# Expert weights split during the feed-forward groups and kept in DRAM, and routing in three batches with row transfers from inside the block

## What is computed

```python
x = x + ffn0(attn0(x))           # L0: 16-head cosine attention; relu^2 feed-forward, 5 spiking steps
X = attn1(x)                     # L1: 16-head attention with a bias, layernorm behind it
X = X + attn_block(rmsnorm(X, g1)) # 4 heads, one shared key and value head
nx = rmsnorm(X, g2);  xf = nx.reshape(-1, d)
rw = softmax(xf @ Wr.T + expert_bias)
topw, topi = top_k(rw, 2);  topw = softmax(topw)
shared = swiglu(xf, sW1, sW2, sW3)
h  = silu(einsum('td,efd->etf', xf, eW1)) * einsum('td,efd->etf', xf, eW3)
eo = einsum('etf,edf->etd', h, eW2)
out = x + X + shared + combine(topw, topi, eo)
```

## Time and profile before

| | us |
|---|---|
| median of three runs | 1443.55 (1443.48 to 1451.34) |
| the profiled execution, as timed | 1444.31 |
| its span, first to last instruction | 1442.6 |
| TensorE busy in the span | 1299.9 (90%) |
| VectorE, ScalarE, GpSimd busy | 1035.3, 896.2, 710.8 |
| DRAM read and written in the span | 39.47 MB, 24.02 MB |

### The profile page before, as it was taken

The page is one execution under the profiler, slowest core; times in us unless marked ns, Lnnn a source line. Parts: engine busy times, 40 slices in busy tenths (PEclk is TensorE's granted clock), DMA queues, the critical chain, the costliest instruction groups (busy, mean ns, idle before and its releaser), DMA issues.

```text
span 1442.6 us, 43140 instructions
## 1 busy us (share of the span) xinstructions
PE 1299.9 (90%) x15310; PEld 1147.9 (80%) x15311; DVE 1035.3 (72%) x2129; ACT 896.2 (62%) x2309; POOL 710.8 (49%) x797
## 2 busy tenths in 40 slices
PE   4899999999689999889999999689998689999990
PEld 4799999998579999778888888568877578888870
DVE  4798988888736555787887787778887576555546
ACT  3676777767356666656666676477776254555545
POOL 2556565564435454445445444367766662333330
PEclk9899999999799999999999999899999899999995
DMA  8200000001030000000000000020001623333319
GB/s 230 54 9 10 8 11 8 8 10 38 2 87 1 1 0 1 3 10 10 9 8 10 9 8 13 21 58 15 16 15 63 221 87 116 104 104 101 103 42 349
DMA packets 87021, 71.15 MB, mean 49 GB/s; under 512 B 49981, under 2 KB 80831, under 8 KB 85824
## 3 DMA queue, kind: packets, MB, share of 16 engines
q1 hardware_dynamic: 80320, 51.73, 12.6%
q0 software_dynamic: 6528, 17.05, 3.3%
HBM read 39.47 MB, written 24.02 MB: 44 GB/s over the span
## 4 chain that ended last, share of the span: by engine, by line
PE 53%; issue 21%; POOL 10%; DVE 9%; ACT 4%; another core or an unknown queue 1%; DMA 1%; DVEq 0%; ACTq 0%; POOLq 0%; SPq 0%
PE psQ L2332 8%; PE psQ L1946 7%; PE psW L2024 7%; PE psW L2311 5%; POOL pn L758 5%; PE psQ L2137 3%; POOL rq L784 3%; PE psS L2137 3%; PE psW L2125 3%; PE psM L2125 3%; PE psS L2048 2%; PE psT L1975 2%; PE psT L2059 2%; PE psM L1998 2%; PE psT L2319 2%
## 5 line engine op out<-in xcount | busy, mean ns | idle before, releaser
L1946 PE MATMUL psQ<-xT,wq 128*128 128x256 f32 x1536 | 225.2, 298 | 3.5 <-ACT cur L1114 1.8
L1946 PEld LDWEIGHTS psQ<-xT,wq 128*128 128x128 f32 x1536 | 205.3, 201 | 4.5 <-issue 2.5
L2024 PE MATMUL psW<-wout,oT 128*128 128x256 f32 x1536 | 205.5, 292 | 1.1 <-ACT oT L977 1.1
L2024 PEld LDWEIGHTS psW<-wout,oT 128*128 128x128 f32 x1536 | 194.3, 197 | 1.3 <-ACT oT L977 1.3
L2332 PE MATMUL psQ<-W,exT 128*128 (+1 forms) x624 | 171.2, 410 | 0.0
L758 POOL TENSOR_TENSOR pn<-ex,rden 128x1024 f32<-128x1024 f32 x64 | 124.5, 1945 | 43.5 <-DVE rden L1437 43.5
L977 ACT ACTIVATE oT<-psT,small 128x512 fp32r<-128x512 f32 x128 | 81.1, 685 | 91.3 <-PE psT L2059 91.2
L802 POOL TENSOR_TENSOR hT<-hf,hT 128x512 fp32r<-128x512 f32 x64 | 85.9, 1341 | 102.1 <-ACT hT L1110 101.9
L912 POOL DMA_INDIRECT results<-result,idx x72 | 70.1, 974 | 133.7 <-ACT result L1241 128.7
L770 POOL TENSOR_TENSOR masked_bias<-bias_t,negmask 128x1024 f32<-128x1024 f32 x32 | 68.9, 2152 | 132.5 <-DVE ex L1405 132.5
L1364 DVE SCALAR_TENSOR_TENSOR oT<-psT,small,oT 128x512 fp32r<-128x512 f32 x128 | 90.2, 746 | 55.9 <-ACT oT L977 55.9
(11 more groups left out here) (302 smaller groups left out, 3374.6 us busy)
## 6 DMA issues: line engine op xcount, KB each, us to landing
rows<-sorted SPq DMA_DIRECT2D x72, 132.0 KB, 2.1
both<-results SPq DMA_DIRECT2D x8, 1024.0 KB, 11.8
raw_w<-W SPq DMA_DIRECT2D x27, 256.0 KB, 3.8
vv<-vp SPq DMA_DIRECT2D x256, 16.0 KB, 1.8
out<-X SPq DMA_DIRECT2D x8, 512.0 KB, 8.8
X<-x SPq DMA_DIRECT2D x1, 3584.0 KB, 18.4
bvv<-v_all SPq DMA_DIRECT2D x128, 16.0 KB, 1.8
sorted<-rows SPq DMA_DIRECT2D x9, 132.0 KB
```

The costliest lines, as they stand in the source:

```text
L1946: mm = nc.tensor.matmul(psQ[:, cc, h * QT:h * QT + QT], wq[w][:, k, c * P:c * P + P], xT[g % 2][u][:, k, :], start=(k == 0 and j == 0), st ...
L2024: mm = nc.tensor.matmul(psW[:, 0:D], oT[u][:, c, :], wout[w][:, c, :], start=(u == 0 and c == 0 and w == 0), stop=(u == 1 and c == CH - 1))
```

## The change

Four things are changed.

**The weights are split early.** The 27 thirds ("pieces") of the nine experts are split on VectorE, both halves, at the end of each of the first six feed-forward groups, 4, 5, 5, 5, 4 and 4 pieces (PARKED). SyncE loads a raw piece (256 KB) into one of four buffers and, once VectorE has split it, writes both halves (512 KB) to the DRAM tensor `parked`; it waits until that write has landed before it loads the next piece into the same buffer. VectorE waits once for all pieces, at the start of the last group. VectorE's loop over the groups is written out. The raw buffers lie in places that the feed-forward doesn't use.

**The experts are loaded split.** `load_expert` is one transfer of 1.5 MB in place of three of 256 KB. Experts 0 and 1 are loaded one after the other, SyncE waiting for the first to land before it goes on to the block's value rows. The 54 split instructions are gone from the block and the shared expert, on ScalarE and VectorE.

**Three batches.** Tiles 0 to 11 are chosen at steps 22 and 23, ranked on TensorE within step 25, ahead of the output product of tile 19 in the same PSUM bank psW, and placed at 25; tiles 12 to 23 at 34, 35, 37 and 37; tiles 24 to 31 at 41, 42, 43 and 44. TensorE's next output product waits until VectorE has read the ranks (`r_read`).

**Row transfers from step 26 on.** One send a step for 14 steps, then the other 50 one after another, held to the shared expert's transposes by `(t - 7) * 8 // 7 + 1`. GpSimd's and VectorE's block loops are written out for it.

```diff
-BATCHES = ((0, 20), (20, TILES))
-FIRST_CHOICE, SECOND_CHOICE, RANK, PLACES = (-6, 5), (-5, 6), (-2, 7), (-1, 8)
-SENT_AHEAD = 3
+BATCHES = ((0, 12), (12, 24), (24, TILES))
+FIRST_CHOICE, SECOND_CHOICE, PLACES = (-14, -2, 5), (-13, -1, 6), (-11, 1, 8)
+RANKED_BEFORE, RANK = (19, 31), 7
+SEND_STEP, SENT_IN_BLOCK = 26, 14
...
-SPLIT_STEP = [-4, -3, -2, 0, 1, 2, 3, 4, 5] + list(range(10, 28))
+PARKED = [4, 5, 5, 5, 4, 4, 0]
+PIECES = KD + 1
...
+            def load_piece(n):
+                p, part = divmod(n, PIECES)
+                raw = raw_piece[n % 4][:, 1, :]
+                got = sem(f"p_raw{n % 4}")
+                if part < KD:
+                    for j, w in enumerate(("W1", "W3")):
+                        sp.dma_start(raw[:, j * D:j * D + D], a[w][p, part * P:part * P + P, :]).then_inc(got, 16)
+                else:
+                    sp.dma_start(raw.rearrange("p (k n) -> p k n", k=KD), a["W2"][p].rearrange("(k p) n -> p k n", p=P)).then_inc(got, 16)
+            def park(n):
+                p, part = divmod(n, PIECES)
+                sp.wait_ge(sem("p_lo"), n + 1)
+                sp.dma_start(parked[p, :, :, part * 2 * D:part * 2 * D + 2 * D], piece[n % 4][:].bitcast(F32)).then_inc(sem("p_kept"), 16)
+                sp.wait_ge(sem("p_kept"), 16 * (n + 1))
+            for n in range(4):
+                load_piece(n)
+            for n in range(PIECES * EP):
+                park(n)
+                if n + 4 < PIECES * EP:
+                    load_piece(n + 4)
             spread_v(LAYERS[1], load_block)
...
+                sp.dma_start(W[:, slot, :, :].bitcast(F32), parked[p]).then_inc(done, 16)
             sp.wait_ge(sem("t_oev"), 2 * TILES)
-            for p in range(2):
-                load_expert(p, SHARED_SLOT + p, sem("e_first"))
+            load_expert(0, SHARED_SLOT, sem("e_weights"))
+            sp.wait_ge(sem("e_weights"), 16)
+            load_expert(1, SHARED_SLOT + 1, sem("e_weights"))
...
-            for p in (3, EP - 1, EP - 2):
-                load_expert(p, (p + 1) % EP, sem("e_rest"))
-            for p in range(4, EP - 2):
-                load_expert(p, p + 1, sem("e_last"))
+            for p in range(3, EP):
+                load_expert(p, (p + 1) % EP, sem("e_weights"))
...
-                if t >= SENT_AHEAD:
-                    pool.wait_ge(sem("e_xTp"), t - SENT_AHEAD + 1)
-                for k in range(TOP_K):
-                    send(t, k)
-            pipeline(pool, block_step, 1, 4, 10, numbers)
+                if n >= SENT_IN_BLOCK and k == 0:
+                    pool.wait_ge(sem("e_xTp"), (t - SENT_IN_BLOCK // TOP_K) * 8 // 7 + 1)
+                send(t, k)
+            for i in range(1, TILES + 10):
+                block_step(i, i % 2)
+                numbers(i)
...
+            def split_piece(n):
+                part = n % PIECES
+                hi, lo = piece[n % 4][:, 0, :], piece[n % 4][:, 1, :]
+                raw = raw_piece[n % 4][:, 1, :]
+                dve.wait_ge(sem(f"p_raw{n % 4}"), (0 if n % 4 else 16) + sum(16 if m % PIECES == KD else 32 for m in range(n % 4, n + 1, 4)))
+                if part < KD:
+                    then(nc.vector.tensor_scalar(hi, raw, g2col[:, part:part + 1], None, ALU.mult))
+                    ins = nc.vector.scalar_tensor_tensor(lo, raw, g2col[:, part:part + 1], hi.bitcast(F32), ALU.mult, ALU.subtract)
...
             ffn_in_lo(0, 0)
+            for g in range(GROUPS):
+                ffn(g, g % 2, first=g == 0, last=g == GROUPS - 1)
+                if g < GROUPS - 1:
+                    for n in range(sum(PARKED[:g]), sum(PARKED[:g + 1])):
+                        split_piece(n)
```

More of the change, by code:

```diff
@@ L335, in build @@
         count = sb("ffn_work", "count", [P, G4 * D], BF16)
+        pieces_at = (place["xT"][0] - 8 * K, place["ffn_work"][0])
+        piece = [nc.alloc_sbuf_tensor_at(f"piece{i}", [P, 2, 2 * D], F32R, offset=pieces_at[i // 2] + 4 * K * (i % 2)) for i in range(4)]
+        raw_piece = [nc.alloc_sbuf_tensor_at(f"raw_piece{i}", [P, 2, 2 * D], F32, offset=pieces_at[i // 2] + 4 * K * (i % 2)) for i in range(4)]
         place["ffn_work"][0] += 8 * K
@@ L407, in build @@
         row_place = sb("route", "row_place", [P, TOP_K, TILES], I32)
-        next_row = [sb("route", f"next_row{i}", [P, E], F32) for i in range(3)]
+        next_row = [sb("route", f"next_row{i}", [P, E], F32) for i in range(4)]
         blank_at = sb("route", "blank_at", [P, E], I32)
@@ L1246, in expert_step @@
                     nc.scalar.activation(ehT[0][:], psT[:, 0, 0:D].rearrange("p (k q) -> p k q", q=P), ACT.Copy).then_inc(sem("e_hhi"), 1)
-            def first_half(i):
-                for piece in range(3 * EP):
-                    if SPLIT_STEP[piece] == i:
-                        split_expert(piece // 3, piece % 3)
             def merged(i):
@@ L1791, in _, with read_ranks, places @@
             ends = end_tile[(E.bit_length() - 1) % 2]
-            def places(b):
-                low, high = BATCHES[b]
-                tiles = slice(low, high)
+            def read_ranks(b):
                 dve.wait_ge(sem("r_ranked"), b + 1)
                 ranks, total = rank_bank(b)
-                then(nc.vector.tensor_tensor(place_of[:, tiles, :], ranks, every_tile(next_row[b][:], b), ALU.add))
+                then(nc.vector.tensor_tensor(place_of[:, slice(*BATCHES[b]), :], ranks, every_tile(next_row[b][:], b), ALU.add))
+                nc.vector.tensor_tensor(next_row[b + 1][:], total, next_row[b][:], ALU.add).then_inc(sem("r_read"), 1)
+                dve.wait_ge(sem("r_read"), b + 1)
+            def places(b):
+                tiles = slice(*BATCHES[b])
+                if b == 2:
+                    read_ranks(b)
                 for k in range(TOP_K):
@@ L1804, in places @@
                 nc.vector.tensor_copy(row_place[:, :, tiles], pos[:, :, tiles]).then_inc(sem("r_placed"), 1)
-                then(nc.vector.tensor_tensor(next_row[b + 1][:], total, next_row[b][:], ALU.add))
             def tile_ends(part):
```

123 lines of the change are left out of this document (48 added, 75 removed).

## The result

The changed kernel takes 1453.42 us (median of 18 runs, 1449.12 to 1456.64), the kernel before 1445.05 (18 runs, 1439.28 to 1451.34): a ratio of 1.0057, 95% interval 1.0046 to 1.0068, that is 8 us slower, clear of noise and under one per cent. The direction was the forecast one, and both the range of 1436 to 1479 and the forecast's own of 1452 to 1473 hold it; the amount was a little under half of the +18 forecast. The two profiled spans are 1442.6 and 1450.4 us.

| from ...

The account below looks back on a forecast made before the run. TensorE was taken to bound the feed-forward and routed tiles, where any wait is paid in full. Feed-forward 16.5, block 1, its start 0.5 and shared expert 0 made +18 on 1444.3: 1462.3 profiled, median 1461.5 us, range 1436 to 1479.

Parts of the forecast that it names:

- The feed-forward: Feed-forward: TensorE stalls before a down product in three groups with five pieces, none with four; +16.5 us, +2 to +26.
- the time of five pieces: Feed-forward: five pieces end 9.7 us after the input's low part, the fifth waiting for the first one's buffer.
- the cover: Feed-forward: the moments can be 5.8 us later before TensorE stands; four pieces hidden, five not.
- the clock: Feed-forward: each of three stalls also lowers TensorE's granted clock, costing 1.6 us more.
- At its start SyncE now has 1.5 MB landing ... +0.5: Block's start: 1.5 MB landing and 1.5 MB more queued ahead of the first value rows cost +0.5 us.
- The block: Block: routing moved to steps 22, 23 and 25, later splits removed and sends earlier; sum +1 us.
- the pauses at steps 30 and 31: Block: routing work leaves these steps, which take 6.4 and 6.0 us where step 29 takes 4.6; -3.2 us.
- the step that divides the 29.2 lost us: Shared expert: loss divided into 4.1, 12.3 over the expert loads, and 12.8 in the last 25 tiles; change's effect 0.
- if the hole over the loads is gone: Shared expert: sign that the prediction is wrong, the 12.3 us hole during the six experts' loads disappearing.
- (a): Feed-forward rival: pieces are hidden, each group loses under 1 us, 16.5 becomes 2, giving 1447 us; chance 0.15.
- (b): Shared expert and block rival: hole doubles, +12 for +5, written-out loops add +5 in pauses, giving 1474 us; chance 0.13.
- (c): Shared expert rival: holes close with long transfers and shorter streams, stage 25.8 us shorter, giving 1436 us; chance 0.22.

Follow-up runs that it names:

- the repeated profile: The changed kernel with no edit, run again in a later set beside the kernel before: 1435.49 us, ratio 1.0027 to the kernel before.
- the early splitting alone: The kernel before with only early splitting, parking in DRAM and loads of split weights; routing and sends as before: ratio 1.0056 to the kernel before.
- the profile without pauses: The kernel before with no edit, profiled again in a later set: 1431.97 us, shared expert's stage 97.87 us.
- the routing alone: The kernel before with only three batches, ranks ahead of the output product and sends from step 26; weights raw, split late: ratio 0.9938.
- the last one: The changed kernel with four pieces a group (three behind the seventh) and experts 0 and 1 loaded in thirds between value rows: 1440.4 us, ratio 0.9972.

## Why the prediction was right and wrong

**The feed-forward: right in its mechanism, place and count, too large by 7.4 us.** Three waits in front of a down product, released by `hT`, none behind four pieces: as forecast. The first wrong term is the time of five pieces, 9.7 us forecast, 8.6, 8.2 and 8.0 measured. Its parts, in the group of 8.6: a write of 512 KB was put at 3.5 us and lands in 3.1 (SyncE's next load is issued 3.13 us behind it); issue and landing of the raw load were put at 0.9 + 2.7 and are 3.0 together; the first and the fifth piece were put at 1.3 each and take 1.3. SyncE's stream, and both transfers from the page of the changed kernel:

```profile
476.49 0.52 SPq L629 DMA_DIRECT2D parked<-piece  x1
479.62 1.37 SPq L621 DMA_DIRECT2D raw_piece<-W  x2
```

```profile
parked<-piece SPq DMA_DIRECT2D x27, 512.0 KB, 3.2
...
raw_piece<-W SPq DMA_DIRECT2D x36, 128.0 KB, 2.1
```

With these times in the forecast's own formula, less the cover of 5.8 us, the waits would be 2.8, 2.4 and 2.2 us; 2.67, 2.25 and 2.04 are measured. The cover was right to 0.2 us. The Trainium skill ("DMA: Bandwidth & Descriptors", Anatomy of one DMA) has a fit for transfers on GpSimd's path, by which the write is 3.2 us, an estimate; this write goes out from SyncE, and its median here is 3.2 too. The second wrong term is the clock, 1.6 us in each of three groups. Here only one of them fell to it: from one `cT` to the next the three groups take 25.9, 27.6 and 25.7 us, where 23.4 is usual. In the repeated profile all three did (27.6, 27.4, 27.4), and the stage was 3 us longer. So the clock's 1.6 us is real, but a wait of 2.0 to 2.7 us sometimes brings it and sometimes not, and the forecast took it as certain. Length doesn't decide it in this range: 2.25 us didn't bring it in the first profile, 2.15 us did in the repeated one. Of the 7.4 us too much, 4.7 are the waits and 3.3 the clock, less small differences.

**The entry: the step "At its start SyncE now has 1.5 MB landing ... +0.5" failed; it is +4.9.** I saw both loads and priced neither the wait in SyncE's stream nor the second load: the value rows aren't issued at all until the first 1.5 MB has landed, 7.37 us, and then they stand behind the other 1.5 and take 7.5 more. For TensorE's down product the prediction asks what is queued behind the waiting instruction; it didn't ask this of SyncE's stream.

**The block: +1.7 for +1 forecast, in part by luck.** Steps 22 to 25 take 6.0 us more where 5.7 to 7.3 was forecast. Behind them, to the first shared product, the forecast had 3.2 us less for the pauses at steps 30 and 31, 4 less for the splits and 1 more for the sends, together -6.2; measured is -1.1 (45.99 + 1.57 before, 43.62 + 2.87 after). Two gains that the forecast didn't have make up for most of it: 1.5 us of the entry's delay come back, and the output products from tile 2 to tile 17 take 70.2 us in place of 71.9. That second gain is in every kernel whose VectorE and GpSimd loops are written out (70.2 to 70.3) and in none of the others (71.7 to 71.9), the early splitting alone among them: some 0.1 us a step, which the forecast put at nothing.

**The shared expert: the step that divides the 29.2 lost us failed.** It gave 0 for the change. Three things were wrong. The loads cost nothing where there are no pauses: full DMA engines and a full TensorE stand side by side in both kernels. By the prediction's own sign, "if the hole over the loads is gone", this part of it was wrong. The splits make 0.5 us of stage and not up to 4. And the row transfers of the kernel before were counted as something that stays inside the stage, when they are a second chain as long as the stage: 64 x 1.28 = 82 us at the least, from 1101.5 on, the last one ending at 1203.7, 10.2 us before the first routed product of the earlier trace rows. In the profile without pauses this distance is 9.9 us, and TensorE waits for it; in the first one the pauses had made TensorE as late as the sends. Rows 10 showed the end of the chain; I read only the price of one transfer from it. So 11.4 of the change's 13.8 us of stage are this wait and the clock behind it, and 7.3 was left of the 13.8 in the first comparison.

**The rivals.** (a), the pieces hidden: falls. (b), the loads weigh by their bytes: falls; the changed kernel has 9.4 MB of them and TensorE at 5.00 of 5. (c), the holes close: its stage of 85.1 us was close to the 83.4 to 84.2 of five profiles in three sets, but not by its mechanism: the routing alone, with the short loads and all the splits, has 84.6. And in the two sets with pauses the changed kernel and the last one kept 103.5 and 103.3. That the sum came out in the range owes something to two errors of opposite sign, +4.4 at the entry against -7.4 in the feed-forward and -7.3 in the shared stage, and to those inside the block. A reader should trust the feed-forward's reasoning and not the total.

## What to carry to other kernels

Before work is moved into an engine's idle time, look at who waits for the instruction that it is put ahead of: nearly ten idle us a group didn't help where one instruction was due within 5.8, and the same work behind that instruction, or one piece less, was nearly free. A wait for a landing in the stream that issues transfers holds back every later one, whatever its size: here 7.37 us for value rows that TensorE needed. And for each engine that feeds the next stage, multiply count by price and compare the end of that chain with the end of the stage; where the two lie close, a gap in the bounding engine's row says nothing on what will set the end once the gap is closed.

## What the runs showed of the hardware

**The same program has pauses in some sets and none in others.** In two sets of runs (kernel before at 1445 and 1446 us) ScalarE and VectorE stand still for 2 to 5.5 us several times in the shared stage, mostly together, with their inputs ready; in the other three sets (1430 to 1432 us) no such wait exists in any of eleven profiles. The expectations above call this a matter of the chip. That isn't shown: the record's number of the chip is 0 for the first set of experiments, without pauses, and for the last, with them, and it doesn't say what else differed. One of the pauses, in the changed kernel of the first comparison, ScalarE and VectorE going on within 0.06 us of each other, on results that TensorE had ended over 7 us before (the transposes at 1127.4, the product at 1127.2):

```profile
1134.73 0.38 ACT L1254 ACTIVATE ehT<-psT 128x256 fp32r<-128x256 f32 x1 [4.62 <-remote]
```

```profile
1134.67 0.42 DVE L1877 TENSOR_TENSOR X<-psW,X 128x256 f32<-128x256 f32 x1 [4.10 <-remote]
```

```profile
1135.62 1.65 PE L2323 MATMUL psW<-W,ehT 128*128 128x256 f32 x6 [4.50 <-issue]
```

```profile
1131.35 0.97 POOL L912 DMA_INDIRECT sorted<-xf_all,row_place  x1 [0.31 <-issue]
1132.62 0.97 POOL L912 DMA_INDIRECT sorted<-xf_all,row_place  x1 [0.30 <-issue]
1133.90 0.97 POOL L912 DMA_INDIRECT sorted<-xf_all,row_place  x1 [0.30 <-issue]
...
1137.82 0.97 POOL L912 DMA_INDIRECT sorted<-xf_all,row_place  x1 [2.94 <-remote]
```

```profile
1137.16 3.29 SPq L642 DMA_DIRECT2D W<-parked  x6
```

In this pause the other two engines only follow. TensorE goes on 0.06 us after VectorE has written the low part of `ehT`, which it needs. GpSimd sends on through the pause at its usual 1.28 us and stops 2.94 us behind it, ahead of the next transfer that is held to the shared expert's transposes; all its stops of 2 us and more, in all three profiles with pauses, stand ahead of such a transfer.

The loads are issued only after this pause, so they aren't its cause. Row transfers run during every pause seen, but they run in the same way in the sets without. The written-out loops aren't it either: the kernel before has pauses without them, and the changed kernel has none with them in its repeated profile. Nor does the number of instruction packets on the page differ, 116 and 62 for the changed kernel in both its profiles, 116 and 57 for the kernel before in both.

```profile
q8 instruction: 116, 1.90, 0.6%
q14 instruction: 62, 0.51, 0.1%
```

That instructions stream in on their own queue and mostly hidden (the Trainium skill, "Runtime: NRT & Kernel Launch", Instruction fetch mechanics) agrees with the profiles without pauses. What the pauses are stays open; the run that held the sends back would have to be made in a set that has them. They lengthen the stage of the kernel before by 13.0 us (97.9 to 110.9), where they also take the place of the wait of 9.60 us for the sends, and that of the changed one by 19.4 (84.1 to 103.5). The difference, 6.4 us, is enough for the change's looking worse, 1.0057, where they occur than where they don't, 1.0027.

**The subtraction of a piece can run long.** It takes 0.69 or 0.75 us, and 1.67 where it meets GpSimd's `ffn_lo` (504.17 to 505.49 and 504.37 to 506.04 in one of them), once in each of the six groups with pieces. It is the one part of a piece that was dearer than forecast; in the groups of five the wait for the fifth piece's data absorbs it.
